# VectorE instead of GpSimd for two raw operand sums (S4q, S1q) in the second group of a Strassen-Winograd attention kernel on one Trainium2 core

## The reference, cut to what matters

```python
h_q = (x @ w_q.T).reshape(b, lq, H, DH)
h_k = (key_value_states @ w_k.T).reshape(b, lk, H, DH)
score = jnp.einsum('bqhd,bkhd->bhqk', h_q, h_k) + position_bias[None]
```

## Time and profile before

| what | value |
|---|---|
| time before, median of 3 runs | 1077.29 us (1076.8 to 1078.42) |
| time of the profiled execution | 1079.05 us |
| its span, first to last instruction | 1076.8 us |
| granted TensorE clock, mean of the span | 0.992 |
| TensorE matmul busy | 1030.2 us, 96% of the span |
| VectorE busy | 761.8 us, 71% |
| ScalarE busy | 500.6 us, 46% |
| GpSimd busy | 472.6 us, 44% |
| share of the chain that ended last: TensorE | 79% |

### The profile page before, as it was taken

How to read it: one execution, slowest core, us unless ns; L and a number is a source line. 1 busy time by engine, 2 the same in 40 slices (tenths; PEclk the granted TensorE clock), 3 DMA queues, 4 the chain that set the end, 5 groups by cost and what they waited for, 6 DMA issues and landing times.

```text
span 1076.8 us, 20565 instructions
## 1 busy us (share of the span) xinstructions
PE 1030.2 (96%) x6354; PEld 894.6 (83%) x6354; DVE 761.8 (71%) x2269; ACT 500.6 (46%) x1377; POOL 472.6 (44%) x567
## 2 busy tenths in 40 slices
PE   7899988999989999999999999999999999999995
PEld 6678767888778888888888888988888888988884
DVE  5799989664747676757677676767676767577883
ACT  4888886453424343534443434444343434343421
POOL 7676676599934232423324242424242424232242
PEclk9999999999999999999999999999999999999998
DMA  4302001235265556473737464646465564736001
GB/s 153 128 12 60 2 1 66 80 126 195 69 227 185 177 180 215 140 238 125 253 135 238 148 222 159 223 170 213 147 217 180 176 221 135 239 110 248 5 20 59
DMA packets 44845, 158.72 MB, mean 147 GB/s; under 512 B 4737, under 2 KB 21505, under 8 KB 32129
## 3 DMA queue, kind: packets, MB, share of 16 engines
q0 software_dynamic: 14240, 103.82, 28.0%
q1 hardware_dynamic: 30560, 54.37, 15.0%
HBM read 148.73 MB, written 9.44 MB: 147 GB/s over the span
## 4 chain that ended last, share of the span: by engine, by line
PE 79%; DVE 10%; issue 4%; POOL 3%; ACT 2%; DMA 2%; POOLq 0%; SPq 0%; DVEq 0%; ACTq 0%
PE bank L1946 25%; PE bank L760 20%; PE bank L2108 16%; PE bank L2095 5%; PE bank L2078 5%; PE bank L2126 3%; PE bank L2085 2%; DVE sm L481 2%; DMA ring<-block_sums 1%; POOL sm L322 1%; DVE alpha L557 1%; DMA stage<-in_wq 1%; ACT pr L1339 1%; PE bank L2164 1%; PE bank L686 1%
## 5 line engine op out<-in xcount | busy, mean ns | idle before, releaser
L1339 ACT ACTIVATE pr<-sm,nmx 128x128 f32<-128x128 f32 x256 | 99.8, 391 | 176.2 <-DVE nmx L1594 172.7
L1048 POOL TENSOR_TENSOR bm<-mask,bias 128x512 f32<-128x512 f32 x64 | 84.5, 1321 | 162.3 <-DVE nmx L1594 159.7
L1644 DVE TENSOR_TENSOR acc<-acc,bank 128x512 f32<-128x512 f32 x128 | 86.2, 684 | 80.1 <-PE bank L2108 80.1
L1077 POOL TENSOR_TENSOR pool_gate<-eps 128x1 f32<-128x1 f32 x95 | 37.6, 396 | 239.5 <-PE bank L1946 239.5
L1946 PE MATMUL bank<-ring,wqk_hi 128*128 128x512 f32 x392 | 111.0, 405 | 7.1 <-DVE wqk_lo L1612 4.1
L1612 DVE TENSOR_TENSOR wqk_lo<-qk_raw,wqk_hi 128x512 fp32r<-128x512 f32 x98 | 106.2, 1085 | 8.5 <-ACT wqk_hi L1369 8.5
L1332 ACT COPY v<-bank 128x256 f32<-128x256 f32 x124 | 45.9, 370 | 128.6 <-PE bank L760 81.8
L2108 PE MATMUL bank<-wo_hi,at_hi 128*128 128x512 f32 x256 | 101.2, 395 | 0.3 <-DVE acc L1644 0.3
L2108 PE MATMUL bank<-wo_hi,at_lo 128*128 128x512 f32 x256 | 100.5, 392 | 0.5 <-DVE at_lo L1606 0.5
L2108 PE MATMUL bank<-wo_lo,at_hi 128*128 128x512 f32 x256 | 100.6, 393 | 0.0
L1606 DVE TENSOR_TENSOR at_lo<-bank,at_hi 128x512 fp32r<-128x512 f32 x64 | 44.0, 688 | 64.5 <-ACT at_hi L1353 64.5
(11 more groups left out here) (296 smaller groups left out, 2611.1 us busy)
## 6 DMA issues: line engine op xcount, KB each, us to landing
ring<-block_sums POOLq DMA_DIRECT2D x96, 1024.0 KB, 5.2
qk_raw<-in_wqk SPq DMA_DIRECT2D x56, 256.0 KB, 5.3
o_raw<-in_wo SPq DMA_DIRECT2D x16, 512.0 KB, 3.3
v_raw<-in_wv SPq DMA_DIRECT2D x15, 512.0 KB, 4.5
block_sums<-stage SPq DMA_DIRECT2D x6, 512.0 KB, 4.1
acc<-in_x POOLq DMA_DIRECT2D x1, 2048.0 KB, 8.1
qk_raw<-in_wqk SPq DMA_DIRECT2D x4, 512.0 KB, 6.3
bias<-in_bias SPq DMA_DIRECT2D x16, 128.0 KB, 2.1
```

Source lines behind the costliest of these rows:

```text
L1048: nc.gpsimd.tensor_tensor(bm[:, s % 2], mask[:, HALF * (s // HG):HALF * (s // HG + 1), :], bias[:, i:i + 1, :].broadcast_to([P, HALF, T]), ...
L1077: nc.gpsimd.tensor_tensor(pool_gate[:, BLOCKS.index(name):BLOCKS.index(name) + 1], eps[:, 0:1], eps[:, 0:1], ALU.add)
L1339: e = nc.scalar.activation(pr[:, s % 2, k], sm[:, s % 2, k], ACT.Exp, bias=nmx[:, s % 2, k:k + 1], accum_out=sums[:, s % 2, k:k + 1])
L1644: nc.vector.tensor_tensor(acc[:, b], acc[:, b], PX[b % 2][:], ALU.add).then_inc(s_acc, 1)
```

## The change

VectorE makes the raw sums S4q and S1q. `q_fourth` moves to the start of VectorE's step s = 2 of group 1, ahead of the lo part of wv and of `masked_scores(6)`; it waits for S3q's split on GpSimd. `q_first` moves to the end of that step, behind the two accumulations. Both keep their four instructions of 128x512, chained with a semaphore (`s_s1q`). GpSimd's `q_first_split` now waits for eight of them, and its last subtraction is two instructions instead of one. The hi part of T2 moves on ScalarE from behind `exps(7)` and `copy_prT` to ahead of `exps(7)`; its lo part moves on VectorE from behind `normalise(7)` to directly behind `masked_scores(7)`, ahead of both sums C11. A drain is put on GpSimd behind its last loop.

```diff
@@ GpSimd
-            def q_fourth():
-                combine(W_, f32(quarter(xnT[0], 1, 0)), area(2), ALU.subtract)
-                combine(W_, W_, f32(quarter(xnT[1], 1, 0)), ALU.add)
-
-            def q_first():
-                combine(area(2), area(2), f32(quarter(xnT[0], 0, 0)), ALU.add)
-                combine(area(2), area(2), f32(quarter(xnT[1], 0, 0)), ALU.add)
-
             def q_first_split():
                 pool.wait_ge(s_q, TILES * SEVEN)
+                pool.wait_ge(s_s1q, 8)
                 hi_of(quarter(xnT[0], 0, 1), area(2))
-                nc.gpsimd.tensor_tensor(quarter(xnT[1], 0, 1), area(2), f32(quarter(xnT[0], 0, 1)), ALU.subtract)\
-                    .then_inc(s_s1q, 1)
+                for c in range(2):
+                    nc.gpsimd.tensor_tensor(quarter(xnT[1], 0, 1)[:, c], area(2)[:, c], f32(quarter(xnT[0], 0, 1))[:, c],
+                                            ALU.subtract).then_inc(s_s1q, 1)
@@
             q_third_split()
-            q_fourth()
-            q_first()
             bias_mask(1, 3, False)
             three_turns(SEVEN)
             q_first_split()
-            pool.wait_ge(s_s1q, 1)
+            pool.wait_ge(s_s1q, 10)
@@
             first_half(NG - 1)
+            pool.drain()
             pool.wait_ge(s_experts_in, 16 * len(EXPERT_INPUTS))
@@ ScalarE, plain_step
+                if s == 3 and seven_next:
+                    hi_op(g + 1, "T2")
                 exps(n, s, first)
@@
                 if s == TILES - 1 and seven_next:
                     copy_prT(n - 1, False)
-                    hi_op(g + 1, "T2")
@@ VectorE
+            x_sums = Chain(dve, s_s1q, 0)
+
+            def q_combine(out, in0, in1, op):
+                for c in range(2):
+                    x_sums.link(nc.vector.tensor_tensor(out[c], in0[:, c], in1[c], op))
+
+            raw_second = [area(2)[:, c] for c in range(2)]
+
+            def q_fourth():
+                dve.wait_ge(s_ready, 2 * BLOCKS.index("S3q") + 2)
+                q_combine(w_part, f32(quarter(xnT[0], 1, 0)), raw_second, ALU.subtract)
+                q_combine(w_part, f32(quarter(xnT[1], 1, 0)), w_part, ALU.add)
+
+            def q_first():
+                q_combine(raw_second, f32(quarter(xnT[0], 0, 0)), raw_second, ALU.add)
+                q_combine(raw_second, f32(quarter(xnT[1], 0, 0)), raw_second, ALU.add)
@@ plain_step
+                if s == 2 and seven_next:
+                    q_fourth()
                 if s == 2:
                     lo(wv, v_raw, s_wv_h, s_wv, g + 2)
@@
                 if s == 3 and seven_next:
+                    lo_op(g + 1, "T2")
                     sum_c11(g + 1, 0)
                     sum_c11(g + 1, 1)
@@
-                if s == 3 and seven_next:
-                    lo_op(g + 1, "T2")
@@
                         accumulate(n, j, (HALF + 2 * s + j) % B)
+                if s == 2 and seven_next:
+                    q_first()
@@ TensorE, product_5
-                    pe.wait_ge(s_s1q, 1)
+                    pe.wait_ge(s_s1q, 10)
```

## The result

The changed kernel takes 1067.28 us (median of 4 runs, 1067.03 to 1067.96) against 1077.05 us of the kernel before (4 runs), a ratio of 0.9907 with a 95% interval of 0.9892 to 0.9923. The profiled execution took 1067.12 us with a span of 1065.3 us.

What follows compares the result with a forecast made beforehand. TensorE was taken as the bound, through two waits between group 1 and group 2. An earlier p6 of w = 1 (-3.4) and a slower clock (+0.2) sum to -3.2 us: 1077.29 to 1074.1 us, range 1071.9 to 1076.5.

Steps and rivals of the forecast that it cites:

- What bounds the kernel: TensorE, busy 96%; two large waits between group 1 and group 2, 4.11 and 2.60 us, the first with slow clock.
- The drain on GpSimd stands before a wait for inputs, where GpSimd idles: 0.: Added drain behind GpSimd's last loop: forecast to change the time by 0.
- GpSimd loses, VectorE gains eight instructions: Sums S4q and S1q: GpSimd loses 13.3 us, its turns end about 288.4; VectorE gains 5.8 us, 0.73 each.
- +0.3: Shift of group 1's last output and of p1 from VectorE's added sums: +0.3 us, bounds 0 to +1.8.
- -5.6: Ahead of p6 of w = 0: TensorE's 4.11 us wait for T2 and its slow clock go, -5.6 us.
- The S2k load takes over: Ahead of p6 of w = 1: load issued at 296.3, TensorE waits 1.9 us, start 3.4 us earlier than before.
- rival A: The forecast itself: the S2k load becomes the wait, gain 2.5 to 4 us; chance 0.50.
- The second wait: TensorE's 2.60 us wait for the S4k load, with its clock, moves along unchanged: 0, bounds -1 to +1.
- From there on all is the old trace, earlier by one constant.: After the wait for S4k, the rest of the timeline only shifts earlier by one constant.
- C's lost clock: Rival: the new wait before p6 of w = 1 also costs clock, gain 1.6 us, 1075.7 us; chance 0.23.
- D's mechanism: Rival: VectorE and GpSimd block each other on their shared path, up to 6.6 us, 1080.5 us; chance 0.07.

Runs made afterwards that it cites:

- e1: The kernel before with only GpSimd's drain added behind its last loop: 1070.58 us, ratio 0.9939.
- e8: The kernel before with GpSimd's loop over groups 2 to 14 cut in two, a drain between the halves and none added at the end: 1078.61 us, one execution.
- e2: The changed kernel without the added drain: 1073.08 us, ratio 0.9970 to the kernel before.
- e4: The changed kernel without the drain and with T2 in its old places, VectorE making S4q and S1q: 1076.80 us, ratio 0.9997 to the kernel before.
- e5: The changed kernel without its main edit: T2's new order and the drain, both raw sums on GpSimd: 1067.45 us, ratio 0.9907 to the kernel before.
- e11: The changed kernel as it is, timed again in another session: 1067.95 us, ratio 0.9909 to the kernel before.
- e3: The kernel before with only T2's hi and lo parts moved ahead, both raw sums on GpSimd, no drain: 1072.02 us, ratio 0.9954.
- e9: The kernel before with T2's hi part alone moved ahead of exps(7), sums on GpSimd, no drain: 1078.07 us, one execution.
- e10: The kernel before with T2's lo part alone moved directly behind masked_scores(7), its hi part in the old place: 1077.81 us, one execution.

## Why the prediction was wrong

**What bounds the kernel.** Right for the passage, incomplete for the whole: I read TensorE's waits, and TensorE's last product ends at 1065.8 of 1076.8 us, so the 8.3 us behind GpSimd's last computed value are in no list of its waits. The rows I rested on, end at 345 us.

**The step that failed** is "The drain on GpSimd stands before a wait for inputs, where GpSimd idles: 0." Its own cost was indeed 0. Its effect was -6.0 us (e1): a drain's length goes with the transfers issued since the last one (e8), so an early one shortens the closing one. I priced the instruction and didn't ask what it takes from a later one. The view by line at the program's end would have shown the 8.68 us. That term is nearly the whole error: -3.2 forecast, -3.5 measured for everything else (e2). That the rest agreed in size is partly luck: the change's main edit, on which my reasons rested, is worth nothing (e4, and e5 beside e11).

**GpSimd loses, VectorE gains eight instructions.** The prices held: 0.72 to 0.73 each (0.73), the turns were done at 286.9, which is 288.0 on the clock of the trace before (288.4), and the product with v of step 2 came 0.8 us later (0.9). These are corrected by 1.1 us, since the self-attention took that much less in this execution and the whole timeline is earlier. The shift of p1, 0.17, was inside "+0.3". But none of this was needed for the gain: e5 has it without the moved sums.

**T2.** "-5.6" for its wait and clock held in the trace; the reason I gave was half wrong. I began with the blocked `nmx` and GpSimd's late turn. e4 removes both (nmx takes 0.19 us, the turns end at 287.8) and gains nothing; e3 keeps both and gains 4.6. T2's place behind the exponentials and normalise was what counted.

**The S2k load takes over.** Right (rival A's mechanism): corrected for the 1.1 us, it was issued at 295.5 (296.3 forecast), and p6 of w = 1 began 4.0 us earlier (3.4). The wait was 1.55 instead of 1.9 us.

**The second wait, "0 (bounds -1 to +1)".** It shrank by 0.4 us, and its clock did not fall, which gave another 1.6: the stretch from p3 of w = 1 to the next product of its kind (321.00 to 329.59 before) is 8.6 us long, and 7.0 after. That isn't the change: of the kernels with the old passage, e9 and e10 were 7.0 there and e1 was 8.6; of the executions of the changed kernel, the first was 7.0 and e11's 8.4. The trace before lies 1.8 us above the median of its runs, so a comparison of these two traces counts the 1.6 and one of medians hardly does.

**"From there on all is the old trace, earlier by one constant."** Nearly: TensorE was 6.9 us earlier from 322.68 on, until a wait of 0.78 us for another load of sums at 621.58, and 5.9 us earlier behind it. Short waits of this kind stand at other places in e1 (0.44 us), e8 (1.24) and e10 (0.49), and in no other trace.

**The rivals.** C's lost clock behind the new wait did not occur, neither behind 1.55 us nor behind 2.13 (e11; 1.00 in both). D's mechanism is there in small (the split's subtraction took 2.93 for 2.65) and decided nothing. I had no rival in which the title's edit is worth nothing and the small edits everything, which is what e3, e4 and e5 show.

## What to carry to other kernels

Read the end of the span engine by engine, closing drains included: if GpSimd issued many transfers, one drain in a stretch where it idles, after the last of them, takes its work off the end; put among loads that are still needed it holds them back (e8). When an operand is late, look first at what stands ahead of it in each of the queues that make it, and move all of its pieces: here each alone gave nothing, both together 4.6 us. Take a change of several edits apart before crediting it, as the largest edit may be worth nothing.

## What the runs showed of the hardware

A closing drain on GpSimd took 8.68 us with 98 transfers issued since the start (before, e2), 4.35 with 45 since the last drain (e8) and 0.66 with none (after, e1), all long landed: near 0.082 us for each. Put right behind the issue of a load, a drain took 9.40 us with 53 (e8); why is open.

How long TensorE waited did not by itself decide whether its granted clock fell behind the wait for S4k. After 2.02 us (e1) the stretch behind it took 8.6 us, after 2.43 us (e8) 7.0, after 2.54 us (e11) 8.4. These 1.4 to 1.6 us come and go between executions with nearly the same wait.
